# Softmax row vectors of an attention and expert layer: from TensorE transposes to DMAs, with a new order of work

## The chip, the cores and the metric

The kernel runs on one core of a Trainium2 chip. The metric is the device time of one execution in microseconds. The core has TensorE (PE, with its weight loads, PEld), VectorE (DVE), ScalarE (ACT) and GpSimd (POOL); SyncE (SP) issues DMAs. Each engine runs its own queue in program order and waits on semaphores.

## The reference, cut to what matters

```python
x = L0_attn_x                      # 8 x 512 x 128
xn = _layernorm(x, axis=-1)
x = x + _L0_attn_ref(xn, W_qkv, W_out) + _L0_ffn_ref(xn, ...)

# _L0_attn_ref: 16 heads of 64, causal, rotary q and k (pairs ::2 and 1::2 are turned)
scores = jnp.einsum('bqhd,bkhd->bhqk', q, k) * scale
weights = jax.nn.softmax(jnp.where(mask, scores, NEG_INF), axis=-1)
out = jnp.einsum('bhqk,bkhd->bqhd', weights, v)

# _L0_ffn_ref: attention with 16 heads of 8 over xn, layernorm, residual,
# a gate over 8 experts, the top 2 of them, layernorm, residual
attn = jax.nn.softmax(scores, axis=-1)
all_out = jnp.einsum('bsd,edf->bsef', x, We) + bexp
```

## The kernel before

The eight batch elements ("batches" from here on) go through one software pipeline. The work is cut into named steps, each of which runs on one engine. A table `START` gives each step of a batch a number, `PERIOD` is added per batch, and each engine's program is its steps sorted by that sum (`ORDER`). The table thus decides only the order on each engine; waits on the semaphores `done[kind]` do the rest. A second table, `PSUM`, says which of the 8 banks a TensorE step writes; `place()` works out who must have read that bank before.

Tokens lie in four tiles of 128 (`T`). Attention's 16 heads go in 8 pairs `c`; in a pair, head 0 is on partitions 0 to 63 and head 1 on 64 to 127. For one pair:

- `proj` (PE) makes q and k transposed, `raw` (ACT) copies them out, `swap` (SP) copies them with the two halves of each rotary pair exchanged (the projection's columns are sorted so that the halves are blocks of 32 partitions: 4 DMAs), `rope` and `lo` (POOL) and `hi` (ACT) turn them and split them into two parts.
- `sm` (PE) makes scores with queries on partitions, in three units, and `max` (DVE) leaves their negated row maxima in `nmax`. `mT` (PE) transposes these: four transposes, so that the maxima of a head stand in one partition of the bank. `row` (ACT) copies the whole bank, 128x512, into `max_row`.
- `st` (PE) makes the scores with keys on partitions, in three units, and adds the maxima row by a fourth product with `pick_row`. `exp` (ACT) and `tri` (POOL, the causal corner) follow.
- `ls` (PE) sums the exponentials into bank rows, `pv` (PE) multiplies them with v. `lsb` (ACT) copies the sums out, `lT` (PE, four transposes) brings queries to partitions, `inv` (DVE) adds two partial sums and takes reciprocals, `fan` (ACT) repeats them 64 times, `rT` (PE, four transposes) turns them back, `rb` (ACT) copies them to `l_wide`, and `div` (DVE) multiplies the bank of `pv` with `l_wide` into `u`. `ao` (PE, after pairs 3 and 7) is the output product.

The second branch has the same shape in 4 groups `g` of 4 heads: `fqk`, `fsm`, `fmax`, `fmT` (four transposes), `fsub` (DVE adds the whole 128x512 bank to the queries), `fst`, `fexp`, `fpv`, then `fT`, `fdiv`, `cT`, `wo`, `x2T`, `gate`, `moe`.

A bank that `pv` wrote is free once `div` has read it, so a later step of PE on that bank waits for `div`, and with it everything behind it in PE's queue.

Of the kernel before, what the change touches and what calls it, by code (L numbers as in the profile page):

```python
# [74 lines left out]
    "fo": [108.396, 146.206, 165.558, 171.894],
    "fT": [106.206, 139.064, 156.304, 162.354],
    "fdiv": [110.608, 138.748, 155.51, 168.461],
    "cT": [170.306],
    "ch": [186.013],
    "cl": [172.273],  # L80
    "wo": [184.847],
    "ln1": [182.239],
    "rs1": [212.863],
    "nm1": [186.736],
    "x2": [214.03],
    "x2T": [203.57],
    "x2h": [224.291],
    "x2l": [204.509],
    "gate": [216.585],
    "gsub": [216.496],  # L90
    "gexp": [243.333],
    "pick": [223.071],
    "moe": [234.735, 238.319, 239.203, 248.291],
    "moew": [228.863, 229.116, 229.719, 236.321],
    "ln2": [244.792],
    "rs2": [264.516],
    "nm2": [254.534],
    "out": [281.989],
    "store": [365.908],
    "load": [366.532],  # L100
    "proj": [-32.459, -19.157, -16.321, -4.8, -1.718, 29.848, 30.714, 44.936, 46.601, 72.717, 82.423, 93.275, 97.88,
        104.304, 107.854, 126.809],
    "raw": [-22.45, -12.503, -9.676, 12.903, 15.041, 46.473, 52.011, 65.297, 70.056, 85.592, 90.651, 94.588, 96.93,
        112.96, 116.612, 139.095],
    "swap": [73.97, 104.111, 118.455, 123.138, 124.789, 149.283, 152.289, 155.734, 171.504, 182.573, 192.436,
        197.939, 202.572, 202.811, 211.666, 233.761],
    "rope": [-15.651, -14.724, 32.189, 34.707, 54.267, 55.422, 62.215, 71.711, 85.177, 90.606, 112.985, 118.722,
        122.991, 125.037, 131.389, 133.101],
    "hi": [4.471, 9.567, 33.103, 39.688, 54.362, 58.189, 80.676, 81.547, 93.143, 93.951, 108.161, 109.474, 129.883,
        133.392, 151.294, 152.598],  # L110
    "lo": [3.711, 18.664, 40.97, 47.924, 59.883, 69.366, 81.127, 84.713, 91.653, 110.934, 119.401, 121.412, 130.883,
        131.248, 133.16, 140.471],
    "v": [35.247, 40.16, 40.169, 42.005],
    "vc": [56.466, 57.439, 59.092, 61.9],
    "sm": [5.12, 8.791, 14.337, 32.061, 34.331, 43.455, 60.849, 61.608, 63.523, 86.995, 94.872, 99.197, 100.462,
        100.895, 101.365, 117.792, 120.861, 126.968, 142.025, 142.347, 142.795, 154.694, 155.905, 156.828],
    "max": [10.32, 12.421, 12.737, 12.935, 13.93, 14.52, 24.453, 25.649, 28.149, 30.693, 39.109, 39.256, 50.793,
# [4 lines left out]
    "row": [38.638, 67.028, 88.897, 103.258, 124.931, 148.842, 154.95, 184.094],  # L122
    "st": [31.553, 34.064, 34.382, 57.05, 60.854, 62.187, 83.416, 90.557, 91.609, 100.63, 100.651, 100.876, 119.572,
        120.591, 122.589, 142.267, 142.735, 142.738, 154.327, 154.73, 155.103, 170.656, 171.741, 172.577],
    "exp": [51.965, 52.299, 54.019, 74.268, 76.176, 80.207, 90.66, 91.851, 94.104, 104.326, 106.931, 107.857, 126.4,
        128.105, 128.825, 150.085, 151.126, 151.248, 159.397, 161.826, 165.472, 190.793, 192.615, 195.277],
    "tri": [61.002, 72.311, 110.915, 121.243, 125.747, 131.813, 146.075, 202.751],
    "ls": [42.275, 67.63, 99.494, 111.628, 127.159, 145.288, 161.584, 190.463],
    "lsb": [62.272, 85.458, 101.044, 122.157, 137.362, 152.125, 171.771, 203.648],
    "pv": [62.358, 94.987, 112.285, 128.938, 141.242, 159.197, 190.65, 201.646],  # L130
    "lT": [46.462, 78.369, 100.383, 117.511, 133.593, 145.971, 162.233, 192.201],
    "inv": [40.074, 66.979, 91.428, 119.181, 135.311, 151.241, 168.208, 187.039],
    "fan": [66.623, 91.796, 110.044, 126.114, 140.533, 157.227, 180.832, 210.049],
    "rT": [57.041, 94.41, 108.744, 124.172, 136.524, 158.095, 170.638, 197.437],
    "rb": [73.937, 93.783, 114.719, 129.322, 144.77, 169.136, 190.781, 216.414],
    "div": [58.994, 81.732, 112.26, 133.525, 138.772, 162.053, 186.753, 202.038],
    "ao": [132.966, 207.322],
    "yadd": [135.044, 205.229],
}

PSUM = {
    "xT": [1],
    "fv": [0],
    "fqk": [5, 6, 2, 5],
# [98 lines left out]
def build(nc, x, w_qkv, w_out, wq, bq, wk, bk, wv, bv, wo, bo, g1, be1, g2, be2, wg, bg, we, bexp, table, rope, out):  # L243
    with ExitStack() as ctx:
# [3 lines left out]
        def sem(name):  # L248
            return ctx.enter_context(nc.semaphore(name))
# [845 lines left out]
```

## Time and profile before

| quantity | value |
|---|---|
| median of 3 runs | 1400.55 us (1398.38 to 1405.91) |
| the profiled execution, its time and its span | 1396.29 us, 1394.6 us |
| PE busy | 1242.4 us, 89% |
| DVE busy | 965.9 us, 69% |
| POOL busy | 827.2 us, 59% |
| ACT busy | 801.2 us, 57% |
| granted TensorE clock, mean | 0.968 |

Busy time is that of an engine's own instructions in the profiled execution; waits on semaphores and the issuing of DMAs aren't in it. The span runs from the first to the last instruction; the execution's time is 1.7 us longer.

### The profile page before, as it was taken

What the parts mean: (1) busy time and instruction counts of PE and PEld (TensorE: products, weight loads), DVE (VectorE), ACT (ScalarE), POOL (GpSimd) and SP (SyncE); (2) the same over time, 40 slices, a digit from 0 to 9 for tenths busy, and PEclk for the clock granted to TensorE, in tenths of its full rate; (3) what the DMA queues carried; (4) which work ended last, traced back from release to release, by engine and by line L of the source; (5) the groups of instructions that cost most, each with busy time, mean ns of one, the idle gap of its engine ahead of it and who ended that gap; (6) DMA issues with size and microseconds to landing.
All of it is one profiled execution on the core that took longest, in us unless ns stands there. A gap on an engine that the chain in (4) does not pass through costs nothing.

```text
span 1394.6 us, 27585 instructions
## 1 busy us (share of the span) xinstructions
PE 1242.4 (89%) x9800; PEld 813.4 (58%) x9800; DVE 965.9 (69%) x2329; ACT 801.2 (57%) x1135; POOL 827.2 (59%) x796
## 2 busy tenths in 40 slices
PE   0688999989999899989998899988999989999994
PEld 0465557655666557756576555765566655775553
DVE  5547656975769658796568955697576975878634
ACT  1366675556655575465855567555665557546660
POOL 0676366772786547592585736667278654759322
PEclk9899999999999999999999999999999999999998
DMA  4111011111111101110011101101011110111000
GB/s 116 44 41 31 16 31 25 31 39 24 24 32 43 28 22 32 25 48 22 18 30 31 46 16 32 31 24 39 24 24 32 40 31 21 33 25 43 12 1 8
DMA packets 38608, 43.04 MB, mean 31 GB/s; under 512 B 10438, under 2 KB 21962, under 8 KB 38348
## 3 DMA queue, kind: packets, MB, share of 16 engines
q1 hardware_dynamic: 35292, 38.33, 11.4%
q10 hardware_dynamic: 3184, 2.95, 0.7%
q8 instruction: 82, 1.34, 0.4%
q14 instruction: 50, 0.41, 0.1%
HBM read 5.60 MB, written 2.10 MB: 6 GB/s over the span
## 4 chain that ended last, share of the span: by engine, by line
PE 48%; DVE 18%; issue 16%; POOL 12%; ACT 3%; SPq 1%; DMA 1%; POOLq 0%; DVEq 0%; ACTq 0%
PE work L922 7%; PE work L947 6%; PE work L835 5%; PE work L1005 4%; PE work L837 4%; PE work L836 4%; PE work L936 3%; DVE work L796 2%; POOL qk_l L449 2%; PE work L898 2%; PE work L977 2%; PE work L968 2%; DVE work L777 2%; DVE fnmax L695 2%; DVE branch L665 2%
## 5 line engine op out<-in xcount | busy, mean ns | idle before, releaser
L695 DVE TENSOR_REDUCE fnmax<-work 128x2 f32<-128x1024 f32 x256 | 303.7, 1218 | 88.4 <-PE work L977 87.0
L524 ACT ACTIVATE fpt<-work 128x1024 f32<-128x1024 f32 x256 | 249.5, 1025 | 98.6 <-PE work L994 97.1
L796 DVE CUSTOM_DVE_ANT_0 work<-work,causal 128x512 f32<-128x512 f32 (+3 forms) x512 | 239.1, 515 | 90.9 <-PE work L898 88.2
L440 POOL TENSOR_TENSOR raw<-raw,cos_t 128x512 f32<-128x512 f32 x128 | 164.1, 1282 | 117.6 <-DMA swapped<-raw 107.4
L457 POOL TENSOR_SCALAR_AFFINE_SELECT pt<-pt 128x256 f32<-128x256 f32 x128 | 49.5, 409 | 298.4 <-ACT pt L573 298.4
L573 ACT ACTIVATE pt<-work 128x1024 f32<-128x1024 f32 (+1 forms) x192 | 164.2, 882 | 61.6 <-PE work L922 60.8
L449 POOL TENSOR_TENSOR qk_l<-raw,qk_h 128x512 fp32r<-128x512 f32 x128 | 163.4, 1285 | 48.9 <-ACT qk_h L555 48.8
L444 POOL TENSOR_TENSOR raw<-raw,swapped 128x512 f32<-128x512 f32 x128 | 164.2, 1283 | 10.0
L441 POOL TENSOR_TENSOR swapped<-swapped,sin_t 128x512 f32<-128x512 f32 x128 | 164.1, 1282 | 0.0
L947 PE MATMUL work<-pt,v 128*64 128x512 f32 (+3 forms) x1024 | 152.0, 439 | 0.5
L549 ACT COPY raw<-work 128x512 f32<-128x512 f32 x128 | 75.7, 592 | 93.0 <-PE work L837 78.5
L1005 PE MATMUL work<-fpt,fv 128*9 128x512 f32 x1024 | 126.6, 594 | 0.0
L947 PEld LDWEIGHTS work<-pt,v 128*64 128x64 f32 x1024 | 67.9, 136 | 81.6 <-issue 62.8
L555 ACT CAST qk_h<-raw 128x512 fp32r<-128x512 f32 x128 | 79.4, 621 | 33.6 <-POOL raw L444 33.6
L922 PE MATMUL work<-qk_h 64*128 64x512 f32 (+3 forms) x512 | 94.8, 360 | 3.3 <-DVE fnmax L695 0.7
L898 PE MATMUL work<-qk_h 64*128 64x512 f32 (+3 forms) x512 | 85.0, 366 | 9.4 <-DVE branch L780 3.4
L994 PE MATMUL work<-fqk 32*128 32x512 f32 x512 | 66.0, 502 | 28.2 <-DVE u L813 26.2
L922 PE MATMUL work<-qk_l,qk_h 64*128 64x512 f32 (+3 forms) x512 | 87.1, 328 | 0.0
L922 PE MATMUL work<-qk_h,qk_l 64*128 64x512 f32 (+3 forms) x512 | 86.6, 326 | 0.0
L922 PE MATMUL work<-max_row,pick_row 64*128 64x512 f32 (+3 forms) x512 | 86.3, 325 | 0.0
L936 PE MATMUL work<-pt,fv 128*32 128x512 f32 (+3 forms) x1024 | 85.6, 446 | 0.0
L813 DVE TENSOR_TENSOR u<-work,l_wide 128x512 f32<-128x512 f32 x64 | 43.9, 687 | 54.7 <-issue 30.1
(165 smaller groups left out, 2606.4 us busy)
## 6 DMA issues: line engine op xcount, KB each, us to landing
swapped<-raw SPq DMA_DIRECT2D x512, 64.0 KB, 2.0
x_in<-in_L_attn_x_dram SPq DMA_DIRECT2D x8, 256.0 KB, 3.3
out_dram<-x_in SPq DMA_DIRECT2D x8, 256.0 KB, 2.3
fpt<-in_L_attn_W_qkv_dram ACTq DMA_DIRECT2D x1, 1536.0 KB, 6.6
pt<-in_L_ffn_We_dram ACTq DMA_DIRECT2D x1, 512.0 KB, 9.4
wout<-in_L_attn_W_out_dram ACTq DMA_DIRECT2D x1, 512.0 KB, 7.2
pt<-in_rope_dram ACTq DMA_DIRECT2D x1, 192.0 KB, 7.6
qk_bias<-in_L_ffn_bq_dram SPq DMA_DIRECT2D x12, 0.1 KB
```

The source lines that it names most:

```text
L440: nc.gpsimd.tensor_tensor(raw[:, n % 3], raw[:, n % 3], cos_t[:], ALU.mult)
L441: nc.gpsimd.tensor_tensor(swapped[:, n % 2], swapped[:, n % 2], sin_t[:], ALU.mult).then_inc(pool_link, 1)
L444: nc.gpsimd.tensor_tensor(raw[:, n % 3], raw[:, n % 3], swapped[:, n % 2], ALU.add).then_inc(done["rope"], 1)
L449: nc.gpsimd.tensor_tensor(qk_l[:, c % 2, k], raw[:, n % 3], qk_h[:, c % 2, k].bitcast(F32), ALU.subtract).then_inc(done["lo"], 1)
L524: nc.scalar.activation(fpt[:, i, 2 * r:2 * r + 2].rearrange("p h n -> p (h n)"), bank_of(("fst", b, g, i), 2 * r, 2), ACT.Exp, scale=1.0 / ...
L573: nc.scalar.activation(pt[:, c % 2, :, PT_UNIT[unit]:PT_UNIT[unit] + ST_N[unit]], scores, ACT.Exp, scale=1.0 / math.sqrt(DH)).then_inc(don ...
L695: nc.vector.tensor_reduce(fnmax[:, j, 2 * r:2 * r + 2, 0:1], bank_of(("fsm", b, g, j), 2 * r, 2).rearrange("p (f n) -> p f n", f=2), AX.X, ...
L796: ins = nc.vector.tensor_tensor_reduce(out=scores, in0=scores, in1=causal[:, S - n:S], scale=-1.0, scalar=3.0e38, op0=ALU.add, op1=ALU.min ...
L922: ins = nc.tensor.matmul(bank_of(x_, h)[:, at:at + S - i * P], lhs, rhs, start=n == 0, stop=n == 3, tile_position=(h * DH, 0))
L936: ins = nc.tensor.matmul(psum[row:row + STRIP, i * P:S], ones, pt[:, c % 2, h, PT_AT[i]:PT_AT[i] + S - i * P], start=n == 0, stop=n == 1, ...
L947: ins = nc.tensor.matmul(psum[h * DH:(h + 1) * DH, i * P:S], v[:, i, 2 * c + h], pt[:, c % 2, h, PT_AT[i]:PT_AT[i] + S - i * P], start=i = ...
L1005: ins = nc.tensor.matmul(psum[f * STRIP:f * STRIP + FVW], fv[:, i, g * GH + f], fpt[:, i, f], start=i == 0, stop=i == T - 1, tile_position ...
```

## The change

Three hand-overs are done by DMA, and every engine's order and the bank table are written anew.

1. Maxima of a pair: `max` packs them into 8 columns, `mT` is one transpose into 8 rows of a bank, `row` copies 8x128 into `rows`, and a new SP step `mrow` copies these to the two partitions of `max_row` that `st` needs. In the second branch `fmT` is one transpose into 16 rows, `fsub` copies 16x128, and `fput` (SP) puts them in the row of `fqk` that was kept for them.
2. Softmax sums: `lT`, `fan`, `rT` and `rb` are gone. After `lsb`, `lc` (SP, 2 DMAs) spreads the sum rows over 128 partitions, 8 values each; `inv` adds and inverts these; `lr` (SP) writes the reciprocals to a scratch in device memory; `lw` (SP) waits for that and reads it back into `l_wide`, each of the two rows of 512 repeated over 64 partitions; `div` waits for `lw`.
3. `swap` moves alternate partitions, 2 DMAs of 64 partitions in the place of 4 of 32; the projection's columns keep their order.
4. `START`, `PSUM` and `PERIOD` have new numbers.

```diff
-    "row": [38.638, 67.028, 88.897, 103.258, 124.931, 148.842, 154.95, 184.094],
+    "row": [175.258, 188.697, 206.775, 221.957, 234.203, 247.7, 258.739, 275.537],
+    "mrow": [131.752, 135.996, 174.622, 189.526, 222.072, 230.86, 235.061, 260.445],
...
-    "SP": ("swap", "store", "load"),
+    "SP": ("swap", "mrow", "lc", "lr", "lw", "fput", "store", "load"),
...
+        r_rows = nc.dram_tensor("r_rows", (2, 2, S), F32, kind="Internal").ap()
...
-                    for p0 in range(0, P, HB):
-                        p1 = p0 ^ HB
-                        sp.dma_start(swapped[p0:p0 + HB, n % 2], raw[p1:p1 + HB, n % 3]).then_inc(swap_done[n % 2], 16)
+                    for r in range(2):
+                        sp.dma_start(swapped[r:P:2, n % 2], raw[1 - r:P:2, n % 3]).then_inc(swap_done[n % 2], 16)
+                elif kind == "mrow":
+                    c = x_[2]
+                    sp.wait_ge(*after("row", b, c))
+                    sp.wait_ge(*after("st", *ring(1, b, c, NC), 2))
+                    sp.dma_start(max_row[0:P:DH].bitcast(F32), m_rows.bitcast(F32)).then_inc(done["mrow"], 16)
+                elif kind == "lc":
+                    c = x_[2]
+                    sp.wait_ge(*after("lsb", b, c))
+                    sp.wait_ge(*after("inv", *ring(1, b, c, NC)))
+                    for n in range(2):
+                        sp.dma_start(l_part[:, n], l_rows[n * STRIP:P:DH]).then_inc(done["lc"], 16)
+                elif kind == "lr":
+                    c = x_[2]
+                    sp.wait_ge(*after("inv", b, c))
+                    sp.wait_ge(*after("lw", *ring(2, b, c, NC)))
+                    sp.dma_start(r_rows[c % 2].rearrange("h (p j) -> (h p) j", p=DH), l_inv[:]).then_inc(done["lr"], 16)
+                elif kind == "lw":
+                    c = x_[2]
+                    sp.wait_ge(*after("lr", b, c))
+                    sp.wait_ge(*after("div", *ring(1, b, c, NC)))
+                    sp.dma_start(l_wide[:], r_rows[c % 2].unsqueeze(1).broadcast_to([2, DH, S])).then_inc(done["lw"], 16)
+                elif kind == "fput":
+                    g = x_[2]
+                    sp.wait_ge(*after("fsub", b, g))
+                    sp.dma_start(fqk[0:P:STRIP, g % 2, 0].bitcast(F32), fm_rows.bitcast(F32)).then_inc(done["fput"], 16)
...
-                    nc.vector.tensor_tensor(fqk[:, g % 2, 0], bank_of(("fmT", b, g)), fqk[:, g % 2, 0].bitcast(F32),
-                                            ALU.add).then_inc(done["fsub"], 1)
+                    dve.wait_ge(*after("fput", *ring(1, b, g, G)))
+                    nc.vector.tensor_copy(fm_rows, bank_of(("fmT", b, g))[0:T * GH, 0:P]).then_inc(done["fsub"], 1)
...
-                    nc.vector.tensor_reduce(l_sum[:].unsqueeze(3), sums, AX.X, ALU.add).then_inc(dve_link, 1)
+                    nc.vector.tensor_tensor(l_sum[:], l_part[:, 0], l_part[:, 1], ALU.add).then_inc(dve_link, 1)
...
-                    for t in range(T):
-                        ins = nc.tensor.transpose(psum[:, tile(t)], nmax[:, t:t + P], ident)
-                    ins.then_inc(done["mT"], 1)
+                    nc.tensor.transpose(psum[0:2 * T, 0:P], nmax[:].rearrange("p h t -> p (h t)"), ident).then_inc(done["mT"], 1)
...
-                elif kind == "rT":
-                    c = x_[2]
-                    pe.wait_ge(*after("fan", b, c))
-                    for t in range(T):
-                        ins = nc.tensor.transpose(psum[:, tile(t)], l_rows[:, tile(t)], ident)
-                    ins.then_inc(done["rT"], 1)
```

Where the order moved. On PE, in the fifth batch, between `mT` of pair 2 and the first unit of `st` of that pair (L908 is `mT`, L955 `lT`, L835 to L839 with `we_h` are the last expert product, with `xt_h` a `proj`, L922 `st`), before (the dots leave out the second half of that product, four like rows):

```order
L908 MATMUL work<-consts,nmax 128x128 x4
L955 MATMUL work<-consts,l_rows 128x128 x4
L835 MATMUL work<-we_h,ct_h 128x512
L836 MATMUL work<-we_h,ct_l 128x512
L837 MATMUL work<-we_l,ct_h 128x512
L839 MATMUL work<-biases,pick_row 128x512
...
L835 MATMUL work<-xt_h,wqkv_h 128x512
L836 MATMUL work<-xt_h,wqkv_l 128x512
L837 MATMUL work<-xt_l,wqkv_h 128x512
L922 MATMUL work<-qk_h 128x512 x2
L922 MATMUL work<-qk_l,qk_h 128x512 x2
L922 MATMUL work<-qk_h,qk_l 128x512 x2
```

After, the same place; `mT` is L921, and L1026 is `x2T`, L992 and L977 steps of the second branch, L959 `pv`, L934 `st`:

```order
L1026 MATMUL work<-consts,xn 128x128 x4
L992 MATMUL work<-fqk 128x512 x4
L921 MATMUL work<-consts,nmax 8x128
L959 MATMUL work<-pt,v 64x512 x2
L959 MATMUL work<-pt,v 64x384 x2
L959 MATMUL work<-pt,v 64x256 x2
L959 MATMUL work<-pt,v 64x128 x2
L977 MATMUL work<-fqk 128x512 x4
L934 MATMUL work<-qk_h 128x512 x2
L934 MATMUL work<-qk_l,qk_h 128x512 x2
L934 MATMUL work<-qk_h,qk_l 128x512 x2
```

`mT` of pair 2 has moved up beside the start of the expert branch, is one transpose, and has `pv` of pair 0 and one step of the second branch behind it before `st`; no L955 or L961 is left. The last unit of this same `st` uses the bank of that `pv`, so it waits for `div` of pair 0.

On SP, before, the queue of that stretch holds `swap` alone (L403), with one store and one load in each batch:

```order
L403 DMA swapped<-raw 32x512 x112
L406 DMA out_dram<-x_in 128x4x128
L409 DMA x_in<-in_L_attn_x_dram 128x4x128
L403 DMA swapped<-raw 32x512 x64
L406 DMA out_dram<-x_in 128x4x128
```

After, at the place of `mrow` of pair 2 in the fifth batch (L411 `swap`, L416 `mrow`, L436 `fput`, L422 `lc`, L427 `lr`, L432 `lw`):

```order
L411 DMA swapped<-raw 64x512 x2
L436 DMA fqk<-rows 4x4x128
L422 DMA l_part<-l_rows 128x1x8 x2
L411 DMA swapped<-raw 64x512 x2
L416 DMA max_row<-rows 2x4x128
L427 DMA r_rows<-l_inv 128x8
L432 DMA l_wide<-r_rows 128x1x512
L411 DMA swapped<-raw 64x512 x4
L422 DMA l_part<-l_rows 128x1x8 x2
L436 DMA fqk<-rows 4x4x128
L427 DMA r_rows<-l_inv 128x8
L416 DMA max_row<-rows 2x4x128
```

Behind `lc` of pair 0 (the first L422) now stand a `swap`, `mrow` of pair 2, then `lr` and `lw` of pair 0; SP takes them in this order, whichever is ready first. The two `swap` steps behind `lw` are for pair 4.

## Rows read from the trace of the kernel before

**Rows 1.** The page, part 1: busy us, share of the span, instructions

```profile
span 1394.6 us, 27585 instructions
PE 1242.4 (89%) x9800; PEld 813.4 (58%) x9800; DVE 965.9 (69%) x2329; ACT 801.2 (57%) x1135; POOL 827.2 (59%) x796
```

**Rows 2.** Busy time of each engine in a middle stretch; clock, DMA share last

```profile
680.00:840.00 160.00, 148.44 (x1182) 97.40 (x1180) 118.57 (x283) 95.50 (x137) 103.21 (x98) 0.98 0.12 29
```

**Rows 3.** The line of `xT`, once a batch: min/median/max ns, first and last start

```profile
L859 PE MATMUL work<-consts,xn x32: 272/273/446, 34.1 to 1134.3; 128*128 128x128 f32 x32
```

**Rows 4.** Who PE waited for, 360 to 1160 us: us, times, longest

```profile
PE work L994 <- DVE u L813: 18.1, 5, 3.7
PE work L835 <- DVE u L813: 12.0, 5, 2.4
PE work L930 <- POOL pt L460: 10.3, 14, 0.9
```

**Rows 5.** PE's timeline: start us, us, instructions; a packed stretch

```profile
708.29 2.38 PE L947 MATMUL work<-pt,v 128*64 128x512 f32 x16
710.60 0.66 PE L908 MATMUL work<-consts,nmax 128*128 128x128 f32 x4
711.09 0.60 PE L955 MATMUL work<-consts,l_rows 128*128 128x128 f32 x4
711.53 0.60 PE L986 MATMUL work<-consts,fnmax 128*128 128x128 f32 x4
711.93 0.50 PE L835 MATMUL work<-xt_h,wqkv_h 128*128 128x512 f32 x1
...
712.83 0.50 PE L977 MATMUL work<-fqk 32*128 32x512 f32 x4
713.26 0.50 PE L835 MATMUL work<-xt_h,wqkv_h 128*128 128x512 f32 x1
...
714.06 0.60 PE L961 MATMUL work<-consts,l_rows 128*128 128x128 f32 x4
714.59 0.50 PE L922 MATMUL work<-qk_h 64*128 64x512 f32 x2
...
715.63 0.40 PE L898 MATMUL work<-qk_h 64*128 64x512 f32 x2
```

**Rows 6.** Groups by line: busy us, mean ns, idle before it

```profile
L813 DVE TENSOR_TENSOR u<-work,l_wide 128x512 f32<-128x512 f32 x64 | 43.9, 687 | 54.7 <-issue 30.1 <-ACT l_wide L590 14.8 <-PE work L947 8.9
L908 PE MATMUL work<-consts,nmax 128*128 128x128 f32 x256 | 43.7, 297 | 7.1 <-DVE fnmax L695 6.7
L955 PE MATMUL work<-consts,l_rows 128*128 128x128 f32 x256 | 41.7, 289 | 0.0
...
L961 PE MATMUL work<-consts,l_rows 128*128 128x128 f32 x256 | 40.4, 280 | 4.0 <-ACT l_rows L584 2.8 <-DVE fnmax L695 1.2
L584 ACT COPY l_rows<-l_inv 128x512 f32<-128x512 f32 x64 | 39.6, 619 | 41.0 <-DVE l_inv L807 40.7
...
L590 ACT COPY l_wide<-work 128x512 f32<-128x512 f32 x64 | 37.6, 588 | 27.5 <-PE work L961 27.0
```

**Rows 7.** The two DVE instructions of `inv`: min/median/max ns

```profile
L804 DVE TENSOR_REDUCE l_sum<-work x64: 158/168/175, 82.0 to 1359.0; 128x8 f32<-128x16 f32 x64
L807 DVE RECIPROCAL l_inv<-l_sum x64: 202/203/204, 82.2 to 1359.2; 128x8 f32<-128x8 f32 x64
```

**Rows 8.** DMA issues: KB each, median us from issue to landing

```profile
swapped<-raw SPq DMA_DIRECT2D x512, 64.0 KB, 2.0
x_in<-in_L_attn_x_dram SPq DMA_DIRECT2D x8, 256.0 KB, 3.3
out_dram<-x_in SPq DMA_DIRECT2D x8, 256.0 KB, 2.3
fpt<-in_L_attn_W_qkv_dram ACTq DMA_DIRECT2D x1, 1536.0 KB, 6.6
```

**Rows 9.** SP's issuing of `swap`: min/median/max ns of one DMA

```profile
L403 SPq DMA_DIRECT2D swapped<-raw x512: 507/590/1920, 39.0 to 1304.0; - x171
```

More of the change, by code:

```diff
@@ L87 @@
[L87 to L102, printed above, removed]
@@ L134 @@
[L134 to L138, printed above, removed]
+    "ln": [56.908],
+    "rs0": [33.307],
+    "xn": [58.66],
+    "xT": [49.918],
+    "xh": [84.601],
+    "xl": [62.382],
+    "fv": [119.07],
+    "fvc": [187.147],
+    "fqk": [88.162, 104.813, 188.833, 213.909],
@@ new lines @@
+    "x2h": [371.245],
+    "x2l": [296.881],
+    "gate": [321.318],
+    "gsub": [308.361],
+    "gexp": [384.031],
+    "pick": [318.806],
+    "moe": [329.132, 334.375, 345.655, 348.266],
+    "moew": [319.489, 321.466, 321.523, 324.194],
+    "ln2": [326.971],
+    "rs2": [342.232],
+    "nm2": [345.369],
+    "out": [358.301],
+    "store": [375.956],
+    "load": [394.932],
+    "proj": [59.766, 60.885, 73.626, 91.827, 101.722, 104.453, 128.677, 137.483, 145.718, 155.214, 162.897, 173.416,
+        198.217, 202.456, 204.04, 218.687],
@@ L139 @@
+    "ao": [212.994, 297.013],
+    "yadd": [228.273, 288.988],
 }
 PSUM = {
[L142 removed]
+    "xT": [5],
     "fv": [0],
[L144 to L155 removed]
[9 rows of a table removed]
+    "fqk": [2, 0, 0, 1],
@@ L165 @@
+    "fsm": [4, 0, 0, 4, 2, 0, 2, 4, 4, 1, 2, 3, 3, 3, 0, 0],
+    "fmT": [6, 6, 0, 3],
+    "fst": [4, 0, 0, 0, 4, 4, 2, 4, 3, 4, 4, 4, 4, 1, 2, 2],
+    "fpv": [0, 7, 0, 7],
+    "fT": [0, 7, 1, 1],
+    "cT": [7],
+    "wo": [2],
+    "x2T": [7],
+    "gate": [5],
+    "moe": [4, 0, 3, 6],
+    "proj": [2, 1, 5, 0, 5, 4, 0, 4, 6, 0, 7, 5, 3, 2, 1, 3],
[7 rows of a table added]
 }
-PERIOD = 166.4394
+PERIOD = 164.7835
 ENGINE = {
     "PE": ("xT", "fv", "fqk", "fsm", "fmT", "fst", "fpv", "fT", "cT", "wo", "x2T", "gate", "moe", "proj", "v", "sm", "mT",
-           "st", "ls", "pv", "lT", "rT", "ao"),
-    "ACT": ("xh", "fvc", "fqkh", "fexp", "fo", "ch", "x2h", "gexp", "raw", "hi", "vc", "row", "exp", "lsb", "fan", "rb"),
+           "st", "ls", "pv", "ao"),
+    "ACT": ("xh", "fvc", "fqkh", "fexp", "fo", "ch", "x2h", "gexp", "raw", "hi", "vc", "row", "exp", "lsb"),
@@ L333, in build @@
         work = ctx.enter_context(nc.psum_tensor("work", [P, BANKS * BANK], F32))
-        done = {kind: sem(f"{kind}_done") for kind in START if kind not in ENGINE["SP"]}
+        r_rows = nc.dram_tensor("r_rows", (2, 2, S), F32, kind="Internal").ap()
+        done = {kind: sem(f"{kind}_done") for kind in START if kind not in ("swap", "store", "load")}
         swap_done = [sem(f"swap{n}_done") for n in range(2)]
@@ L563, in _ @@
                     act.wait_ge(*after("mT", b, c))
-                    act.wait_ge(*after("st", *ring(1, b, c, NC), 2))
-                    nc.scalar.copy(max_row[:], bank_of(("mT", b, c))).then_inc(done["row"], 1)
+                    act.wait_ge(*after("mrow", *ring(1, b, c, NC)))
+                    nc.scalar.copy(m_rows, bank_of(("mT", b, c))[0:2 * T, 0:P]).then_inc(done["row"], 1)
                 elif kind == "exp":
@@ L913, in _ @@
                         pe.wait_ge(*after("lo", b, c, 1))
-                        pe.wait_ge(*after("row", b, c))
+                        pe.wait_ge(*after("mrow", b, c))
                     for i, at in ST_UNITS[unit]:
@@ L990, in _ @@
                     if i == 0:
-                        pe.wait_ge(*after("fsub", b, g))
+                        pe.wait_ge(*after("fput", b, g))
                     for f in range(GH):
```

204 lines of the change are left out of this document (81 added, 123 removed), and 27 rows, old and new, of tables (PSUM, START).

## The prediction

> **What bounds the kernel now.** I read the page's first part, then busy time in a middle stretch, then the waits of the busiest engine, last its timeline. PE is busy 89% of the span [rows 1] and 148.4 of 160 us in the middle, where DVE has 118.6, POOL 103.2 and ACT 95.5 [rows 2]. So PE sets the pace, and leaves 11.6 us in 160 unused. `xT` starts at 34.1 us in the first batch and at 1134.3 us in the eighth [rows 3], so a batch takes 1100.2/7 = 157.2 us; 34 us before and 260 us after are filling and draining. What PE waits for is mostly `div`: 18.1 + 12.0 us between 360 and 1160 us, which is 5.1 batches, so 5.9 us a batch; next is `tri`, 10.3 us or 2.0 a batch [rows 4]. In the timeline one step starts when the last has been fed in, so the price of a step on PE is the distance to the next start: `pv` 2.31 us, `mT` 0.49, `lT` 0.44, `fmT` 0.40, `rT` 0.53, a step of the second branch 0.43, `proj` 0.80, the first unit of `st` 1.04 [rows 5].
>
> **What is taken off PE.** A batch loses 8 `lT` and 8 `rT`: 8 x (0.44 + 0.53) = 7.8 us. The 12 `mT` and `fmT` go from four transposes to one; one alone I put at 0.15 us, a little over a quarter of the group's price, so 8 x 0.34 + 4 x 0.25 = 3.7 us. Together 11.5 us a batch. Busy time by group would give more, (0.75 x 43.7 + 41.7 + 40.4 us) / 8 = 14.4 us without `fmT` [rows 6], but it counts the overlapping ends of matmuls. If no wait grew, 157.2 would become 145.7 and the program some 90 us shorter. ACT loses `fan` and `rb`, 0.62 and 0.59 us each [rows 6], and most of `row`; it is not the bound, so this is worth only the time in a chain. The same holds for `fsub` on DVE.
>
> **What the maxima cost.** Before, `st` could start after `mT` and a copy of about 0.6 us. Now it is `mT`, a small copy (0.2 to 0.3, below the 0.59 of a wide one [rows 6]), a DMA that lands 2.0 us after its issue, as the smallest timed transfer does [rows 8], and three hand-overs of about 0.1: 2.6 to 2.9 us. PE's work between `mT` and `st` in the new order, priced by rows 5: 2.7 us for pair 2 (`pv` and one branch step, as the order shows), 2.2 for pair 7, 3.5 and 3.8 for pairs 0 and 6, 5.4 or more for the rest. Two pairs are short by up to 0.7 us, two are at the edge when ACT is busy. I take 2 us a batch; bounds 0 and 5. In SP's queue `mrow` never stands behind a step that is ready later by these prices, so the queue itself costs it little. The second branch has 3.6 us or more between `fmT` and `fst`: nothing.
>
> **What the sums cost.** The chain from the end of `ls` to the end of `div` was copy 0.59, `lT`, sum and reciprocal 0.37 [rows 7], `fan` 0.62, `rT` 0.53, `rb` 0.59, `div` 0.69 [rows 6]: about 4 us with hand-overs. Now: copy 0.6; two DMA issues, 0.6 until the second goes out [rows 9], and 2.0 to land [rows 8]; sum and reciprocal 0.4; the write of the reciprocals 2.3, as the store's [rows 8]; the wide load; `div` 0.7; seven hand-overs 0.7. That is 7.3 us and the wide load.
> The wide load is the disputed price. It writes 256 KB. Nearest in size and direction is the load of x, 3.3 us [rows 8]. But that one has 128 rows on both sides, and this one has a source of two rows, read 64 times each; no transfer in the trace has such a source. If as few engines carry it as its source has rows, two, each moves 128 KB. The load of W_qkv moved 1536 KB with 16 engines, 96 KB each, in 6.6 us [rows 8]; taking 2.0 us off as fixed, 4.6/96 = 0.048 us per KB, so 128 KB take 6.1 and the landing 8.1 us, an estimate. Bounds: 2.3 (all engines, like a store) and 10. I take 8.1, as no row with a wide source can stand for one with two rows. So the chain is 15.4 us; with 3.3 it would be 10.6.
> Against this stands PE's work from the end of `ls` to the step that reuses the bank of `pv` and so waits for `div`. For pair 0 it is: `pv` 2.3, two `proj` 1.6, four branch steps 1.7, four units of `st` 3.8, three of `sm` 0.95, `x2T` and `mT` 0.6, together 11.0 us. For pairs 1 to 7 the same count gives 17.0, 30.5, 12.2, 17.9, 12.2, 22.7, 17.4. Pair 0 is short by 4.4, and its `lr` stands behind `mrow` of pair 2, which waits for `mT` of pair 2, some 2.4 us more: 6 after what other stalls give back. Pair 3 is short by 3.2 (`ao` waits). Pair 5 is short by 3.2, and its `lw` must wait for `div` of pair 4, which ends late too: 6. For pairs 6 and 7 SP issues `lr` only behind `lc` of pair 7, the two chains run one behind the other, and I put 3. Together 18 us a batch, against the 5.9 of `div` before, which stood at other places and go.
>
> **What costs nothing.** `swap` issues 2 DMAs in the place of 4, so its last one goes out 1.2 us sooner [rows 9], while twice the bytes may land later; both lie on POOL's path, 103 of 160 us busy [rows 2]. New DMAs on SP are 44 a batch, old ones fall from 64 to 32: 76 issues of 0.59 us, 45 us of 157. The wait of `lw` for `lr` adds 8 x 2.3.
>
> **Sum.** A batch: -11.5 (PE) -5.9 (old waits for `div`) +18 (new ones) +2 (maxima) = +2.6 us, seven times 18. Filling and draining happen once: -11.5, +11.4 for one uncovered chain of sums (15.4 for 4), +2 for maxima: +2. From 1396.3 us of the profiled execution, which lies 4.3 below the median of the runs, 1416; against the median, 1420.
>
> **A rule that bears on the wide load.** The Trainium skill, "DMA: Bandwidth & Descriptors", section "Why a DMA increments its semaphore by 16 and not by 1", says that a transfer is dealt to as many engines, at most 16, as divide the outermost count of both its sides; by it this source of two rows gets two engines. No row of this trace shows it. The sum by it is the one above; without it, the first rival's.
>
> **Rivals.**
> - The wide load lands like the load of x, in 3.3 us. It decides below about 4.5 us, where pairs 3 and 5 are covered. Then only pair 0 is late, 1.5 to 2 us: -11.5 -5.9 +2 +2 = -13.4 a batch, and some of the freed time returns as waits that PE's work hid, above all `sm` to `mT`, where four pairs have 1.2 us between them: +4. Seven times -9.4 and -5 at the ends: 1326 us. For it: the size. Against: the source. Chance 0.27.
> - The wide load also holds up what comes behind it: `swap` for pair 4 is issued just behind it, and `lr` of pair 7 behind `lw` of pair 6. If each of 8 loads delays PE by a further 0.8 us through POOL or SP, it is 6 a batch, 1465 us. For it: two transfers on the same engines share them. Against: `proj` to `sm` has 9 us or more of work, 20 mostly. Chance 0.17.
> - It comes out even: the transposes' gain and the waits cancel within 0.5%, since the count of short pairs is off by one. Chance 0.1, 1400 us.
> My forecast has 0.46.
>
> **Numbers.** 0.5%, 7 us, is about what a measurement of this kernel tells from no change. The forecast, 1420, has a range of its own of 1380 to 1460: a landing of 6 us takes 2 off four pairs, about 40 in all; one of 10 adds as much. With the rivals, 1320 to 1470 leaves out 2 in 10. Faster: 0.27 from the first rival and 0.08 from the forecast's low end, 0.35; same: 0.04 and part of the even case, 0.11; slower: 0.54.
>
> **What would show it.** Transposes L955 and L961 gone, PE's busy time 90 to 115 us lower; in the DMA issues `l_wide<-r_rows` at 8 us, `max_row<-rows` at 2.0; waits of PE for `div` at about 18 us a batch, longest 6; `xT` every 160 us. The forecast is wrong if `l_wide` lands in under 5 us, if PE waits for `div` no more than before, or if PE's granted clock, 0.98 in the middle [rows 2], falls.

## The result and the profile after

The changed kernel takes 1635.8 us, the median of four runs (1628.4 to 1642.5), against 1400.5 us: a ratio of 1.167, 95% interval 1.161 to 1.173. I had forecast 1420. The direction was right, the size was off by a factor of twelve.

The page of the changed kernel, parts 1, 2 and 4, whole lines with others left out:

```profile
span 1640.8 us, 25962 instructions
...
PE 1274.8 (78%) x9000; PEld 773.4 (47%) x9000; DVE 924.8 (56%) x2332; ACT 715.4 (44%) x1007; POOL 825.7 (50%) x795
...
PEclk9888899888888988899898888889898998988886
...
PE 36%; DMA 32%; DVE 18%; issue 5%; SPq 3%; ACT 3%; POOL 3%; POOLq 0%; DVEq 0%; ACTq 0%
DMA l_wide<-r_rows 26%; DMA r_rows<-l_inv 6%; PE work L968 5%; PE work L849 5%; PE work L1003 4%; PE work L934 4%; PE work L851 3%; PE work L850 3%; DVE fnmax L710 3%; DVE work L811 3%; PE work L977 2%; PE work L912 2%; PE work L948 2%; DVE u L827 2%; DVE branch L680 2%
```

PE has 800 instructions fewer than in [rows 1] and is nevertheless busy 32 us longer. The row of its clock reads mostly 8. The chain that ended last goes through the wide load (`l_wide<-r_rows`) for 26% of the span.

The same middle stretch as [rows 2], now in the changed kernel, and its line of `xT`, which answers to [rows 3]:

```profile
680.00:840.00 160.00, 129.37 (x919) 75.93 (x918) 93.69 (x237) 71.04 (x100) 79.56 (x74) 0.90 0.12 38
```

```profile
L873 PE MATMUL work<-consts,xn x32: 270/272/448, 34.0 to 1324.1; 128*128 128x128 f32 x32
```

A batch takes (1324.1 - 34.0) / 7 = 184.3 us, before 157.2. So the seven steady batches cost 190 us, and what lies before the first and behind the last `xT` costs 350.7 us in the place of 294.4, another 56. I had priced the two at 18 and 2.

Whom PE waited for in 940 us, 5.1 batches, of the changed kernel:

```profile
PE work L849 <- DVE u L827: 40.1, 9, 5.6
PE work L934 <- DVE u L827: 28.7, 5, 6.3
PE work L992 <- DVE nmax L811: 21.4, 5, 4.6
PE work L968 <- DVE u L827: 16.1, 5, 3.5
PE work L977 <- DVE u L827: 14.9, 5, 3.5
PE work L977 <- DVE fnmax L710: 11.1, 5, 2.3
PE work L849 <- DVE fnmax L710: 11.1, 5, 2.4
```

The four rows of `div` (`DVE u`) make 99.8 us, 19.6 a batch; the forecast had 18. The part of `ao` (L968), 3.2 a batch, is also what the forecast gave it. The others are waits that [rows 4] has not or has small. Between 360 and 1160 us all of PE's waits together are 142.8 us (17 rows, these kinds first), which is 32.9 a batch; before they were 53.1 us (13 rows, the first three are [rows 4]), 10.4 a batch.

The groups of the division and of POOL's first rotary step (busy us, mean ns | idle before it), and the DMA issues that answer to [rows 8]:

```profile
L472 POOL TENSOR_TENSOR raw<-raw,cos_t 128x512 f32<-128x512 f32 x128 | 163.5, 1278 | 324.0 <-DMA swapped<-raw 323.7
...
L827 DVE TENSOR_TENSOR u<-work,l_wide 128x512 f32<-128x512 f32 x64 | 44.3, 691 | 277.7 <-DMA l_wide<-r_rows 277.7
```

```profile
swapped<-raw SPq DMA_DIRECT2D x256, 128.0 KB, 2.2
...
x_in<-in_L_attn_x_dram SPq DMA_DIRECT2D x8, 256.0 KB, 7.6
...
out_dram<-x_in SPq DMA_DIRECT2D x8, 256.0 KB, 5.4
```

Transfers that the change doesn't touch got slower: the load of x from 3.3 to 7.6 us, the store from 2.3 to 5.4. POOL's wait for swapped tiles grew from 107.4 us, in the line of the kernel before, to 323.7 us:

```profile
L440 POOL TENSOR_TENSOR raw<-raw,cos_t 128x512 f32<-128x512 f32 x128 | 164.1, 1282 | 117.6 <-DMA swapped<-raw 107.4
```

One wide load in the timeline (start us, us, engine, line; in brackets the idle time before it and what ended it):

```profile
93.29 0.57 SPq L432 DMA_DIRECT2D l_wide<-r_rows  x1
...
93.98 1.15 SPq L411 DMA_DIRECT2D swapped<-raw  x2
...
101.07 0.69 DVE L827 TENSOR_TENSOR u<-work,l_wide 128x512 f32<-128x512 f32 x1 [4.96 <-DMA l_wide<-r_rows]
...
101.83 1.28 POOL L472 TENSOR_TENSOR raw<-raw,cos_t 128x512 f32<-128x512 f32 x1 [5.34 <-DMA swapped<-raw]
```

The division starts 7.8 us after the load's issue, where I had estimated 8.1. But the swap issued 0.7 us behind it was also used only 7.8 us after its own issue, and its median is 2.2. It had been held up.

How many DMA engines work in that time can be read too. The last but one number is their busy share, of 16:

```profile
98.00:100.00 2.00, 0.00 (x0) 0.00 (x0) 0.00 (x0) 0.00 (x0) 0.00 (x0) 0.64 0.13 43
```

0.13 x 16 is 2.1. So on the average two engines work, and 14 stand idle, while both the load and a swap are still out. This is the count that the forecast had taken from the shape of the source.

### The profile page after: what moved, and what is told of

It reads as the page before. It is cut to its first block, busy times and chain, and to the rows that moved or that the text cites. A ratio compares the mean times of both kernels' runs of the same rounds, so it can differ in the third digit from the quotient of the medians.

```text
span 1640.8 us, 25962 instructions
## 1 busy us (share of the span) xinstructions
PE 1274.8 (78%) x9000; PEld 773.4 (47%) x9000; DVE 924.8 (56%) x2332; ACT 715.4 (44%) x1007; POOL 825.7 (50%) x795
## 4 chain that ended last, share of the span: by engine, by line
PE 36%; DMA 32%; DVE 18%; issue 5%; SPq 3%; ACT 3%; POOL 3%; POOLq 0%; DVEq 0%; ACTq 0%
DMA l_wide<-r_rows 26%; DMA r_rows<-l_inv 6%; PE work L968 5%; PE work L849 5%; PE work L1003 4%; PE work L934 4%; PE work L851 3%; PE work L850 3%; DVE fnmax L710 3%; DVE work L811 3%; PE work L977 2%; PE work L912 2%; PE work L948 2%; DVE u L827 2%; DVE branch L680 2%
## 5 line engine op out<-in xcount | busy, mean ns | idle before, releaser
L472 POOL TENSOR_TENSOR raw<-raw,cos_t 128x512 f32<-128x512 f32 x128 | 163.5, 1278 | 324.0 <-DMA swapped<-raw 323.7
L959 PE MATMUL work<-pt,v 128*64 128x512 f32 (+3 forms) x1024 | 155.8, 447 | 0.0
L1003 PE MATMUL work<-fpt,fv 128*9 128x512 f32 x1024 | 144.9, 646 | 1.2 <-ACT fpt L555 1.2
L934 PE MATMUL work<-qk_h 64*128 64x512 f32 (+3 forms) x512 | 95.3, 366 | 51.4 <-DVE u L827 45.3
L912 PE MATMUL work<-qk_h 64*128 64x512 f32 (+3 forms) x512 | 93.0, 406 | 37.9 <-ACT qk_h L586 10.5
L977 PE MATMUL work<-fqk 32*128 32x512 f32 x512 | 72.4, 552 | 63.5 <-DVE u L827 24.8
L466 POOL TENSOR_TENSOR rstd<-spread,power 128x4 f32<-128x4 f32 x24 | 24.5, 1020 | 185.8 <-DVE spread L675 185.6
L959 PEld LDWEIGHTS work<-pt,v 128*64 128x64 f32 x1024 | 69.0, 139 | 85.3 <-issue 71.5
L948 PE MATMUL work<-pt,fv 128*32 128x512 f32 (+3 forms) x1024 | 101.4, 514 | 0.0
L992 PE MATMUL work<-fqk 32*128 32x512 f32 x512 | 70.6, 538 | 38.9 <-DVE nmax L811 35.0
L968 PE MATMUL work<-wout,u 128*128 128x128 f32 x512 | 78.2, 325 | 23.8 <-DVE u L827 23.8
```

The costliest lines, as they stand in the source:

```text
L472: nc.gpsimd.tensor_tensor(raw[:, n % 3], raw[:, n % 3], cos_t[:], ALU.mult)
L934: ins = nc.tensor.matmul(bank_of(x_, h)[:, at:at + S - i * P], lhs, rhs, start=n == 0, stop=n == 3, tile_position=(h * DH, 0))
L959: ins = nc.tensor.matmul(psum[h * DH:(h + 1) * DH, i * P:S], v[:, i, 2 * c + h], pt[:, c % 2, h, PT_AT[i]:PT_AT[i] + S - i * P], start=i = ...
L968: ins = nc.tensor.matmul(psum[:, tile(t)], u[:, n, tile(t)], wout[:, half * (NC // 2) + n], start=n == 0, stop=n == NC // 2 - 1)
L1003: ins = nc.tensor.matmul(psum[f * STRIP:f * STRIP + FVW], fv[:, i, g * GH + f], fpt[:, i, f], start=i == 0, stop=i == T - 1, tile_position ...
```

## The experiments

Four questions: what part of the 235 us is the wide load's landing, and by which way does it harm; what the other two parts of the change cost; what the order is worth; and what the clock does.

**The wide load in two parts.** Each half has one source row, read by 64 partitions.

```
-  sp.dma_start(l_wide[:], r_rows[c % 2].unsqueeze(1).broadcast_to([2, DH, S]))
+  for h in range(2):
+      sp.dma_start(l_wide[h * DH:(h + 1) * DH], r_rows[c % 2][h:h + 1].broadcast_to([DH, S]))
```

> The changed kernel, with the wide load of the reciprocals issued as two DMAs, each reading one row for 64 partitions, in the place of one DMA that reads two rows. Theory A (the one load is carried by two engines, takes 7 to 8 us, and through div and the granted clock is the whole loss): div starts about 3 us after the issue, PE's waits for div fall from 20 us a batch to under 6, the granted clock returns from 0.87 to about 0.97, and the time is 1310 to 1350 us. Theory B (the order and the DMA hand-overs as such are too late, whatever the load takes): the time stays above 1500 us and the clock below 0.92. Theory C (part and part): 1380 to 1450 us.

1408.9 us (10 runs), ratio 1.005, 1.002 to 1.008, in the range of Theory C: the clock comes back only to 0.93, and not to 0.97 as Theory A had it. Its DMA issues, its line of `xT`, POOL's wait, and the DMA engines while a wide load and a swap are out:

```profile
l_wide<-r_rows SPq DMA_DIRECT2D x128, 128.0 KB, 2.9
```

```profile
L874 PE MATMUL work<-consts,xn x32: 270/272/446, 34.3 to 1126.8; 128*128 128x128 f32 x32
```

```profile
POOL raw L473 <- DMA swapped<-raw: 190.4, 50, 8.9
```

```profile
95.50:97.00 1.50, 1.30 (x18) 1.14 (x18) 1.44 (x2) 0.90 (x2) 1.50 (x2) 1.00 0.71 197
```

The two transfers land 2.9 us after their issue, and the first division starts 3.9 us after the first of them went out (94.1 to 98.0), where with one transfer of the same bytes it was 7.8. The share of 0.71 is 11 engines of 16. That one edit takes away 227 of the 235 us. A batch takes (1126.8 - 34.3) / 7 = 156.1 us, 1.1 less than before; filling and draining take 310 us, 16 more than before.

**Division that doesn't wait.** The load stays as it is in the changed kernel, but `div` multiplies by a table that is always there. The output lacks the softmax's division. On SP a load now waits for the load before it, in the place of the division before it.

```
-  dve.wait_ge(*after("lw", b, c))
-  nc.vector.tensor_tensor(u[...], bank_of(("pv", b, c)), l_wide[:], ALU.mult)
+  nc.vector.tensor_tensor(u[...], bank_of(("pv", b, c)), cos_t[:], ALU.mult)
```

> The changed kernel, where div multiplies by the cosine table and no longer waits for the wide load; the load is still made, and nobody reads it. The output lacks the division by the softmax sums in the first branch. Theory A (PE loses its time waiting for div): 1310 to 1360 us, clock about 0.97, although the load still holds two DMA engines for 6 us each time. Theory D (the load does its harm by holding up the strip exchange behind it on the same engines, and so POOL): above 1480 us, with POOL still waiting over 250 us for the exchanged strips.

1504.8 us, ratio 1.072, 1.066 to 1.077, as Theory D had it. No engine that computes waits for the load any more (SP does, 15.5 us in all), and the kernel is still 104 us slower than before:

```profile
POOL raw L473 <- DMA swapped<-raw: 288.5, 58, 12.1
```

Without the division's waiting 131 us of the loss are gone. The other 96 (1504.8 less 1408.9) come from the load in another way, and perhaps somewhat more, as the kernel with the quick load still waits 4.4 us a batch for `div`. That 131 and 96 make 227 is arithmetic and confirms nothing; the next two runs look for the 96 by themselves.

**A spare load behind each quick one.** To the kernel with the load in two parts one more load is added, which nobody waits for: 192 KB from two source rows in one transfer, or the same bytes in two transfers of one source row. (The spare tile has 384 columns, as there was no room for 512. SP asks before each spare load whether the last has landed; in the list of its waits this never appears.)

```
+  sp.dma_start(extra[:], r_rows[c % 2][:, 0:3 * P].unsqueeze(1).broadcast_to([2, DH, 3 * P]))
```

```
+  for h in range(2):
+      sp.dma_start(extra[h * DH:(h + 1) * DH], r_rows[c % 2][h:h + 1, 0:3 * P].broadcast_to([DH, 3 * P]))
```

> The kernel with the wide load in two parts (1408.9 us), and behind each of its 64 wide loads one more load that nobody waits for: 384 of the 512 columns of both rows onto a spare tile of 128 partitions, as one transfer with two source rows. Theory A (a transfer with two source rows keeps two of the engines busy for some 5 us, and the swaps that are issued behind it wait for those two, so that GpSimd gets its swapped tiles late; division is not touched): GpSimd's wait for swapped tiles grows from 190 us towards 290, and the time goes to 1470 to 1510, near the run whose divisions didn't wait (1504.8). Theory B (the harm of the wide load was its landing time alone, which divisions waited for; who else uses the two engines doesn't matter): 1409 to 1420.

> The same spare load with the same bytes, but as two transfers of one source row onto 64 partitions each. Theory A (two engines are what holds the others up, not the bytes): each load is over in some 2.5 us and every engine shares it, so 1409 to 1425. Theory B (the bytes or the issue of another DMA on SP's queue count): within 15 us of the run with the spare load of two rows in one transfer.

One transfer: 1505.2 us, ratio 1.073, 1.070 to 1.077. Two transfers: 1412.6 us, ratio 1.008, 1.005 to 1.010. POOL's waits in the first and then in the second:

```profile
POOL raw L481 <- DMA swapped<-raw: 288.8, 61, 12.3
```

```profile
POOL raw L482 <- DMA swapped<-raw: 209.3, 51, 9.3
```

The timeline of the first, around one spare load, and its DMA engines in two of these microseconds:

```profile
94.57 1.16 SPq L437 DMA_DIRECT2D l_wide<-r_rows  x2
...
95.76 0.54 SPq L440 DMA_DIRECT2D extra<-r_rows  x1
...
96.42 7.54 SPq L413 DMA_DIRECT2D swapped<-raw  x4
...
98.16 0.69 DVE L836 TENSOR_TENSOR u<-work,l_wide 128x512 f32<-128x512 f32 x1 [0.77 <-DMA l_wide<-r_rows]
...
103.19 1.29 POOL L481 TENSOR_TENSOR raw<-raw,cos_t 128x512 f32<-128x512 f32 x1 [5.43 <-DMA swapped<-raw]
```

```profile
99.00:101.00 2.00, 1.58 (x16) 0.84 (x16) 1.18 (x5) 1.32 (x3) 0.00 (x0) 1.00 0.13 39
```

The division runs 3.6 us after its load's issue, and the swap issued behind the spare load is used 6.8 us after its own. Theory A holds on both runs. A transfer with two source rows that nobody waits for costs 96.3 us, 1.5 each; the same bytes from single rows cost 3.7, less than the spread of the runs. The 96.3 is close to the 96 that the run before had left open. As the spare load has only three quarters of the bytes, it is partly luck that they agree so closely. So neither the bytes nor the added issue does the harm, but the few engines that one such transfer occupies, two by the share of 0.13, and which the transfers behind it on SP's queue need too. Another queue was not tried.

How it reaches PE: `xT` goes from 34.2 us to 1215.8, so a batch takes 168.8 us, 12.7 more than without the spare load. PE's waits between 360 and 1160 us are 98.8 us, 20.8 a batch for 14.4. Those for the maxima and for `xn`, for which the load of x must land, grew most, from 5.0 and 1.5 us:

```profile
PE work L1001 <- DVE nmax L820: 17.7, 4, 4.7
PE work L882 <- DVE xn L689: 13.9, 4, 5.0
```

The other 6.3 us of a batch are PE's own instructions, at a granted clock of 0.91 for 0.95 in that stretch.

The Trainium skill, "DMA: Bandwidth & Descriptors", section "Why a DMA increments its semaphore by 16 and not by 1", says that the outermost counts of both sides decide how many engines carry a transfer; by that, two rows give two engines. The trace agrees, with a busy share of 0.13. The table in the section "Rules for kernel authors" of the same page of the Trainium skill advises against splitting a transfer into halves of the partitions, as both halves use all 16 engines anyway. Here the whole used two, and the measurement says the opposite: 1408.9 us split, 1635.8 whole.

**The swap alone,** on the kernel before: one DMA for each parity of the partitions, and the weights and angles laid out to match.

```
-  for p0 in range(0, P, HB):
-      p1 = p0 ^ HB
-      sp.dma_start(swapped[p0:p0 + HB, n % 2], raw[p1:p1 + HB, n % 3])
+  for r in range(2):
+      sp.dma_start(swapped[r:P:2, n % 2], raw[1 - r:P:2, n % 3])
```

> The kernel before, with the strip exchange alone changed to two DMAs of alternate partitions. Theory A (it costs nothing): within 0.5% of before, 1394 to 1407 us, POOL's wait for the strips falls from 107 us. Theory B (twice the rows in one DMA land later than four small DMAs): 1410 us or more, the median landing above 2.6 us.

1396.1 us (10 runs), ratio 0.996, 0.994 to 0.998.

```profile
swapped<-raw SPq DMA_DIRECT2D x256, 128.0 KB, 2.0
```

Twice the bytes land in the same 2.0 us as in [rows 8]. POOL's wait for swapped tiles did not fall as expected, 108.2 us for 107.4. This part costs nothing, and this kernel is the fastest of all that ran, by 0.4%.

**The maxima alone,** on the kernel before with the order that it has on PE, ACT, DVE and POOL, once with `mrow` in SP's queue and once issued by ACT right behind the copy. SP's queue was ordered anew in both, `swap`, store and load too, and not the same way: the second has its store and load later.

```
+  sp.dma_start(max_row[0:P:DH].bitcast(F32), m_rows.bitcast(F32)).then_inc(done["mrow"], 16)
```

```
+  act.wait_ge(*after("row", b, c))
+  act.wait_ge(*after("st", *ring(1, b, c, NC), 2))
+  act.dma_start(max_row[0:P:DH].bitcast(F32), m_rows.bitcast(F32)).then_inc(done["mrow"], 16)
```

> The kernel before, with the hand-over of the maxima alone changed to one transpose, a small copy and a DMA, in both branches; the order of every other engine is that of before. PE loses 3.7 us of work a batch by my prices. Theory A (the DMA's 2 us are mostly covered, two or three pairs short by about 1 us): 1375 to 1400 us, clock 0.96 or more. Theory B (the order of before has 1.2 to 3.9 us between mT and st, which a chain of 2.9 us overruns in most pairs): 1410 to 1450 us, clock below 0.96, and waits of PE's st for the DMA.

> The kernel before, with the maxima of both branches handed over by DMA as in e3_max_only, but the DMA of a pair's maxima is issued by ACT itself, right behind its copy, so that it can't stand behind a store or a strip exchange in SP's queue. Theory A (e3's loss was the queue: mrow behind the store, 13 us once a batch): 1390 to 1430 us, PE's longest wait for the maxima under 4 us. Theory B (the DMA's own 2 us in an order that gave the hand-over 1.2 to 3.9 us): above 1480 us still.

On SP 1572.5 us, ratio 1.122, 1.118 to 1.127, far above both theories; on ACT 1492.2 us, ratio 1.063, 1.061 to 1.066, Theory B. The worst place of the first:

```profile
675.81 0.39 SPq L420 DMA_DIRECT2D out_dram<-x_in  x1
...
681.80 0.57 SPq L413 DMA_DIRECT2D max_row<-rows  x1
...
683.55 0.80 PE L933 MATMUL work<-qk_h 64*128 64x512 f32 x2 [13.28 <-DMA max_row<-rows]
```

`mrow` stood in SP's queue behind the store, which waits for `out` of the batch before, and behind swaps; PE waited 13.3 us, once a batch. With ACT issuing it, what is left is PE's wait for the transfer itself, 21.3 us between 360 and 1360 us in 22 waits of 1.3 at most, 18.0 us for the rows that `fput` moves, and above all waits for `div`, 54.7 us at one place. How much of the 80 us between the two runs is the issue by ACT and how much the other places in SP's queue is open. In the changed kernel no wait of PE for `max_row` is in its list at all: the new order gives the hand-over its time.

**The sums alone,** on the kernel before and its order outside SP, with the quick load; and **all three parts in the old order,** with the quick load and `mrow` on ACT. The places of the new SP steps are worked out from the times at which the trace of before has `ls`, `inv` and the rest.

```
-    "lT": ..., "rT": ..., "fan": ..., "rb": ...
+    "lc": ..., "lr": ..., "lw": ...
```

> The kernel before, with the softmax sums alone handed over by DMA, the wide load as two DMAs of one source row each; the order of PE, ACT, DVE and POOL is that of before without the four steps that go, and SP's steps stand by the times of the trace of before. PE loses 7.8 us of work a batch. Theory A (with a quick load the chain of about 10.5 us fits into the 15 to 23 us that the old order has between ls and the step that waits for div): 1340 to 1385 us, clock 0.95 or more. Theory B (what leaves PE as work comes back as waits and as a lower clock): 1390 to 1420 us, clock below 0.95.

> All three hand-overs of the change in the old order of PE, ACT, DVE and POOL: maxima as in e7_max_act, sums as in e5_sums_only, strips as in e4_swap_only. To be held against e1_wide16, 1409 us, which has the same hand-overs in the new order. Theory A (the new order was made for the DMAs and is the better one): 1430 us or more. Theory B (the new order has shorter slacks all over and is the worse one): 1330 to 1395 us.

The sums alone: 1608.4 us, ratio 1.146, 1.143 to 1.148, some 190 above the range of either theory. All three in the old order: 1658.9 us, ratio 1.184, 1.181 to 1.187, Theory A. Whom DVE waited for in the first, and whom in the second:

```profile
DVE l_sum L810 <- DMA l_part<-l_rows: 174.2, 32, 10.7
```

```profile
DVE l_sum L815 <- DMA l_part<-l_rows: 143.7, 32, 9.4
```

A load of 4 KB is awaited for up to 10.7 us, so it was issued late: it stands in SP's queue behind swaps that aren't ready, and DVE stands at `inv` with everything behind it. With the same three parts and the same quick load, the new order gives 1408.9 and the old one 1658.9. The chain of four hand-overs by DMA didn't fit the old order with SP's steps as I placed them. How much of these 250 us is the order of PE, and how much the places that I gave SP's steps, is open: the new order with the old hand-overs by PE was not tried.

**Idle products.** Eight products of 64 by 256 are added behind each of the 64 `mT`, once to the changed kernel and once to the one with the load in two parts. Their result is overwritten.

```
+  for n in range(8):
+      nc.tensor.matmul(psum[DH:P, 2 * P:4 * P], ident[:, 0:DH], causal[:, 0:2 * P], start=True, stop=True, tile_position=(0, DH))
```

> The changed kernel, with eight idle products (64 x 256 columns, f32) behind each mT, written to a quarter of that bank which nobody reads: about 1.5 us of work 8 times a batch, nearly 100 us in all, that computes nothing. Theory A (TensorE's granted clock fell because PE stood still so much, and busier it is granted more): the clock rises above 0.89 and the time stays within 15 us of the changed kernel's 1636. Theory B (the clock is no part of it, and PE's work is on the path): clock 0.87, the time grows by 50 to 100 us.

> The kernel with the wide load in two parts and the eight idle products behind each transpose of the maxima, as they were added to the changed kernel, where they cost 31 us. Theory A (with the quick load TensorE is the bound again, at a granted clock of 0.93 already, so that added products can win back little): the clock rises to 0.95 or more, and the time grows by much more than 31 us, to 1460 to 1520. Theory B (the low clock is what keeps this kernel from being faster than the one before, and a busier TensorE wins it back): 1390 to 1420.

On the changed kernel: 1667.1 us, ratio 1.189, 31 us more than without; that is between the two theories, with the clock as Theory A had it. On the other: 1558.3 us, ratio 1.111, 149 us more than without, above the range of Theory A, as the products are dearer than I had priced them. PE, PEld, DVE, ACT and POOL and the clock between 360 and 1160 us, in the order: before, changed, changed with products, load in two parts, that with products:

```profile
360.00:1160.00 800.00, 744.06 (x5912) 491.23 (x5910) 589.32 (x1395) 474.07 (x677) 499.43 (x473) 0.97 0.12 30
```

```profile
360.00:1160.00 800.00, 653.31 (x4689) 393.55 (x4685) 473.81 (x1181) 366.55 (x519) 430.86 (x411) 0.88 0.11 37
```

```profile
360.00:1160.00 800.00, 729.30 (x5131) 443.60 (x5131) 470.45 (x1165) 364.88 (x515) 424.24 (x404) 0.94 0.11 36
```

```profile
360.00:1160.00 800.00, 724.27 (x5486) 444.03 (x5484) 568.62 (x1410) 429.82 (x610) 506.69 (x481) 0.95 0.14 45
```

```profile
360.00:1160.00 800.00, 762.17 (x5459) 461.92 (x5459) 488.19 (x1222) 388.85 (x546) 443.87 (x421) 0.97 0.12 39
```

Work that costs 149 us where PE sets the pace costs 31 where PE waits. Part of the difference fills idle time: PE's waits in this stretch fall from 142.8 to 69.5 us. Another part is the clock, which rises from 0.88 to 0.94. The price of the products and the two lines of `xT` tell the parts apart:

```profile
701.27 3.67 PE L923 MATMUL work<-causal,consts 128*64 128x256 f32 x16
704.87 0.50 PE L849 MATMUL work<-we_h,ct_h 128*128 128x512 f32 x1
```

```profile
L873 PE MATMUL work<-consts,xn x32: 270/272/447, 34.2 to 1348.8; 128*128 128x128 f32 x32
```

```profile
L874 PE MATMUL work<-consts,xn x32: 270/272/447, 34.1 to 1260.1; 128*128 128x128 f32 x32
```

The products behind one `mT` take 3.6 us and not 1.5, so 28.8 us a batch. A batch of the changed kernel grows by only 3.5 us, from 184.3 to 187.8. Its waits give 16.6 of that back (32.9 to 16.3). The remaining 8.7 us are the other instructions, which are the same as without products and take that much less at a clock of 0.94 for 0.88. With the quick load a batch grows by 19.0 us, from 156.1 to 175.1; the waits give 6.6 (14.4 to 7.8) and the other instructions 3.2, at 0.97 for 0.95. So the clock follows PE's idle time: it is low where PE waits and comes back when the gaps are filled, and it has a price of its own.

## Why the prediction was right or wrong

- **The wide load, 8.1 us:** right (7.8), and with it the waits for `div`, 19.6 us a batch for the 18 of the sum. The rule on engines, read before any row showed it, gave the right price.
- **The swap, nothing:** right by itself, 0.4% faster. **The maxima, 2 us a batch:** not visible as a wait in the new order; in the old one they cost some 90 us even by the better queue.
- **PE's work, -11.5 us a batch:** somewhat too high. The kernel with the quick load shows it best: a batch is 1.1 us shorter although its waits are 74.0 us in the stretch for 53.1, 14.4 a batch for 10.4. What isn't waiting fell by 5.1 us. It was run at a clock of 0.95 for 0.97; a share of time s at half clock gives a mean of 1 - s/2, so 10% of a batch for 6%, some 3 us of work lost. That makes about -5 to -8. The sign that PE's busy time would be 90 to 115 us lower failed with the clock: it is 32 us higher, as slower instructions count as longer busy.
- **The step that failed is the sum.** It added the new waits for `div` to a pace that was otherwise left as it was: "Sum. A batch: -11.5 (PE) -5.9 (old waits for `div`) +18 (new ones) +2 (maxima) = +2.6 us". The measured +27.1 a batch has two terms that it lacks. First, other waits of PE: 32.9 a batch for 10.4 are +22.5, of which `div` is 13.7 (19.6 less 5.9) and the rest 8.8. Of the rest 5.5 are there with the quick load too (14.4 less 4.4, against 10.4 less 5.9), so they belong to the new order and the other hand-overs and not to the wide load. Second, PE's own instructions got slower. The changed kernel and the one with the quick load run the same PE instructions. Outside of waits a batch takes 151.4 us in the first and 141.7 in the second, 9.7 more, at clocks of 0.88 and 0.95. Against before the balance is +22.5 for waits and +4.6 for the rest, and the rest is the -5 of the freed work with 9.7 on top. That these 9.7 are the clock is borne out by the idle products, which raise it and win 8.7 back. The Trainium skill, "TensorE: Matmul & The Clock Gate", section "Part 1: The HAM clock gate", says that TensorE runs at half rate unless it is kept busy; the rows agree, 0.97 with 10 us of waiting in 157, and 0.88 with 33 in 184. I had named a falling clock as something that would make the forecast wrong, and given it no price. The range had a slip of its own: 2 us less landing on four pairs is 8 a batch, so nearer 60 us in all than the 40 that I wrote.
- **The ends, +2 us:** measured 56. While the last batch runs, no next batch's work covers its eight chains of sums; I had counted one chain. From the last `xT` to the end it is 316.7 us (1640.8 less 1324.1), before 260.3 by [rows 1, 3]. How the 56 divide between these chains and the clock was not worked out. The clock in the last stretch, 0.79 in the changed kernel and 0.96 before:

```profile
1440.00:1640.00 200.00, 137.35 (x935) 84.28 (x931) 93.86 (x253) 63.68 (x88) 69.57 (x68) 0.79 0.08 25
```

```profile
1200.00:1394.00 194.00, 165.19 (x1319) 108.93 (x1315) 122.74 (x328) 95.34 (x135) 97.26 (x96) 0.96 0.08 19
```

- **The rival of the load that lands quickly, 1326 us:** with 2.9 us, below its threshold, most waits for `div` go, 19.6 us a batch down to 4.4 (it had 2), but its price was 83 us too low. The threshold of 4.5 us itself was not tested. It had freed time come back as 4 us of waits a batch and -5 at the ends; measured were 1.1 gained a batch and 16 lost at the ends. Hiding most of the DMA chain only brings the kernel back to where it was.
- **The rival of the load that holds up what is behind it, 1465 us:** the mechanism is there as it was told, by two experiments. Its price was half of the true one, 1.5 us a load for 0.8, and it isn't an alternative to the forecast but comes on top. Of the 227 us that splitting the load gives back, 131 go with the division's wait and 96 with the engines' release.

## What to carry to other kernels

Before a hand-over is moved to DMA, look at the outermost count of both sides: a transfer from two rows is slow itself and holds up the transfers behind it on its queue, and here splitting it by rows cost one issue and repaired both. When new waits on TensorE are added up, price two more things, the clock that falls while it idles, and the first and last batch, where no other work covers the chain. And an order made for one set of delays is no neutral ground for testing parts of a change: the maxima alone (1492.2 us) and the sums alone (1608.4) were worse in the old order than all parts in the new (1408.9); the swap alone was not.

## What the runs showed of the hardware

- One transfer of 256 KB with two source rows: 7.8 us from issue to use, with a busy share of the 16 engines of 0.13, so two of them; two transfers of 128 KB with one row each: 3.9 from the first issue to use, 2.9 from issue to landing, with a share of 0.71 beside a swap.
- A swap of 128 KB issued 0.7 us behind the first kind is used after 7.8 us in the place of some 2.2; the load of x has a median of 7.6 us in that kernel, 6.3 with spare loads of two rows, 3.6 with spare loads of single rows.
- The median landing of a swap doesn't depend on its size here: 64 KB and 128 KB both take 2.0 us.
- The same PE instructions take 9.7 us a batch more (151.4 for 141.7, waits left out) at a clock of 0.88 for 0.95, and 8.7 less when idle products raise it from 0.88 to 0.94.
- 512 added products cost 149 us at a clock of 0.95 and 31 us at 0.88 with idle time beside it.
